# Query and key pieces batch by batch, last expert rows as high and low products, ten idle products at the gate

## The chip, the cores and the metric

One Trainium2 chip, one core. The metric is device time of one execution in microseconds. The engines run side by side and meet at semaphores: TensorE (PE; PEld is its weight load), VectorE (DVE), ScalarE (ACT), GpSimd (POOL), and SyncE (SP), which only issues DMAs here.

## The reference, cut to what matters

1024 tokens of width 256 (two batches of 512) go through two layers. Layer 0 has attention whose 16 heads use unrotated halves and rotated copies of low-rank queries and keys, then a mixture of 16 gated experts. Layer 1 has a gated delta rule, then this mixture of 12 experts, three per token:

```python
for e in range(E):
    sel = top_idx == e
    mask = sel.any(axis=-1)
    cnt = sel.sum()
    w_e = jnp.sum(jnp.where(sel, ew, 0.0)) / jnp.maximum(cnt, 1).astype(ew.dtype)
    h = jax.nn.relu(jnp.einsum('bsh,hi->bsi', x, w1[e]) + b1[e])
    h = jnp.einsum('bsi,ih->bsh', h, w2[e]) + b2[e]
    out = out + mask[..., None].astype(x.dtype) * (w_e * h)
pooled = out.mean(axis=1)
phi = jax.nn.sigmoid(jax.nn.relu(pooled @ Wp1 + bp1) @ Wp2 + bp2)
phi_mask = (phi > 0.7).astype(out.dtype)[:, :, None]
return out * (1.0 - phi_mask * 0.8)
```

An expert's weight is one number, the mean gate of all its tokens. The pooled mean over a batch decides a factor on all its rows.

## The kernel before, in words

Each engine runs its own list of instructions, in the order in which the program writes them; a wait holds everything behind it on that engine.

**Start.** TensorE computes the latents batch by batch (L1163), then eight up-products (L1168 to L1171) in the order of operands 0, 2, 1, 3: unrotated queries, unrotated keys, and their swapped partners. ScalarE copies operands 0 and 2 out (L830). Score products run in bf16 on three pieces of every fp32 number: ScalarE writes the high piece (L821), VectorE the remainder (L1784), ScalarE the middle piece (L825), VectorE the low one (L1788), each over both batches at once. SyncE writes the six piece arrays to DRAM (L546 to L553), waits for all six, and reads them back in the row order that the heads need; ScalarE issues batch 0's query rows (L837). VectorE makes the swapped operands (L1778) and GpSimd the rotation (L690, L692), whose pieces follow the same way. TensorE computes the value products (L1176) and then, once VectorE has read the swapped operands out of PSUM, the modulation of both layers (L1188), which ScalarE copies (L840) and TensorE turns (L1194). Six idle products (`warm`, bf16, 512 columns each) stand before the first score product (L1211). VectorE reduces each score tile to row maxima (L1819).

**Gate.** Behind layer 1's attention, VectorE computes gate logits, the top three, ranks, and a table of token per slot. TensorE adds the gates of each expert over all tokens (L1623, the gate product), VectorE turns them into expert weights and multiplies these into the one-hot table of experts per token (L2414), TensorE transposes that table (L1626), two idle products, and the expert loop begins. The loop has 35 tiles of 128 slots: GpSimd gathers the tokens' rows (L775), TensorE transposes them (L1634), multiplies up (L1645) and down (L1655) in fp32, VectorE adds the bias and clips (L2450) and scales by the expert weight (L2425), GpSimd scatters the rows to DRAM (L781). Down-product r waits for the scaled rows of r - 1, and VectorE's list has the scaling of r - 1 ahead of the activations of r.

**Tail.** The last two tiles aren't scattered. TensorE adds them, and the bias b2 by the transposed table, into PSUM by fp32 products with one-hot matrices (L1660, L1687). SyncE loads the three z rows of every token back (L667) once all scatters have landed, and VectorE adds PSUM and the three rows per pair of token tiles (L2463, L2465, L2466). TensorE pools (L1695), and the small head (L1700, L1703) and the last scaling follow.

F32R is an fp32 number rounded for TensorE; a product in it takes one instruction where fp32 takes two. Layer 0's mixture already uses it with a high and a low part (L1332).

Of the kernel before, what the change touches and what calls it, by code (L numbers as in the profile page):

```python
# [60 lines left out]
NLAST = 2  # L61
# [73 lines left out]
def program(nc, a, out):  # L135
    with ExitStack() as ctx:
# [12 lines left out]
        x_tok = sb("x_tok", [P, NT, D])  # L149
        hT = sb("hT", [P, KD, TOK])  # L150
# [276 lines left out]
        wmT = carve(TOK)  # L427
# [4 lines left out]
        last_hot = arena[:, at[0] - NP1 * P // 2 - NP1 * NT1:][:, 0:NLAST * TOK].rearrange("p (n t k) -> p n t k", n=NLAST, t=NT)  # L432
        assert NLAST * TOK <= NP1 * P // 2 + NP1 * NT1
# [22 lines left out]
        assert at[0] <= ARENA  # L456
# [70 lines left out]
        def _(sp):  # L527
# [35 lines left out]
            parts_out(1)  # L563
# [112 lines left out]
        def _(pool):  # L676
# [11 lines left out]
            for n in range(2):  # L688
                for b in range(B):
# [3 lines left out]
                                       ALU.add).then_inc(s["rotated"], 1)  # L693
            for n in range(2):
                pool.wait_ge(s["part1"], n + 3)
                pool.tensor_tensor(rest[2 * n + 1], X[:, 2 * n + 1, :], pieces[:, 2 * n + 1, 0, :],
                                   ALU.subtract).then_inc(s["rest1"], 1)
            for n in range(2):
                pool.wait_ge(s["part2"], n + 3)
                pool.tensor_tensor(pieces[:, 2 * n + 1, 2, :], rest[2 * n + 1], pieces[:, 2 * n + 1, 1, :],  # L700
                                   ALU.subtract).then_inc(s["part3"], 1)
            pool.wait_ge(s["parts_out0"], 16 * 6)
# [90 lines left out]

        @block.scalar
        def _(act):
# [24 lines left out]
            def first_piece(t):  # L820
                act.activation(pieces[:, t, 0, :], X[:, t, :], ACT.Copy).then_inc(s["part1"], 1)  # L821

            def second_piece(t, count):
                act.wait_ge(s["rest1"], count)
                act.activation(pieces[:, t, 1, :], rest[t], ACT.Copy).then_inc(s["part2"], 1)  # L825

            for n in range(2):
                for b in range(B):
                    act.wait_ge(s["up"], 2 * n + b + 1)
# [4 lines left out]
            for n in range(2):  # L834
# [9 lines left out]
            for n in range(2):  # L844
                second_piece(2 * n + 1, n + 3)
# [1760 lines left out]
```

## Time and profile before

| | us |
|---|---|
| timed runs | 832.76, 833.20, 840.58 |
| their median | 833.2 |
| the profiled execution | 831.77 |
| its span, first to last instruction | 829.9 |

What lies around the span is 1.87. Rows of a timeline give the start and the duration in us, engine, line, operation, output and inputs with shapes, how many were merged (x), and in brackets the idle time before and what ended it.

### The profile page before, as it was taken

Reading aid. Unit: us, or ns where it says so; the run is one execution under the profiler, and the core shown is the slowest. Engines: PE = TensorE matmul, PEld = TensorE weight load, DVE = VectorE, ACT = ScalarE, POOL = GpSimd, SP = SyncE. Lnnn points to the kernel's source line nnn. Section 1 sums busy time; section 2 is a strip of 40 time slices with the busy share of each in tenths; the row PEclk is TensorE's granted clock in tenths of the full one; section 3 lists DMA queues with packets and bytes.
Section 4 is the critical chain, followed back from the end, with each engine's and each line's share of the span. In section 5 each row is a group of like instructions: output and inputs, shape, how many; then the busy total and the mean of one; then the engine's idle time right before and its main releaser. Section 6 shows DMA issues by size and latency. Waiting matters only on the chain. (4 is left out here: it accounts for less than half of the span.)

```text
span 829.9 us, 11442 instructions
## 1 busy us (share of the span) xinstructions
PE 762.5 (92%) x3982; PEld 560.9 (68%) x3982; DVE 538.8 (65%) x1312; ACT 265.2 (32%) x414; POOL 215.6 (26%) x187
## 2 busy tenths in 40 slices
PE   5899999989999999999999498998957999999995
PEld 4422333477788888887456387777734999999985
DVE  4599996458555544455799999998666443434336
ACT  2455778343334434343571111121231000000000
POOL 4470000032223222231030000976002344444410
PEclk9989999979999999999999799999976999999997
DMA  8695000110111111140022405200015899999953
GB/s 293 154 210 96 2 2 3 39 39 20 58 38 57 38 57 38 57 153 1 25 90 77 190 1 171 59 1 1 1 51 189 310 351 344 335 347 346 337 191 109
DMA packets 38516, 101.17 MB, mean 122 GB/s; under 512 B 5294, under 2 KB 18278, under 8 KB 37510
## 3 DMA queue, kind: packets, MB, share of 16 engines
q1 hardware_dynamic: 34470, 91.06, 33.9%
q0 software_dynamic: 3552, 9.11, 2.9%
q10 hardware_dynamic: 448, 0.39, 0.2%
q8 instruction: 27, 0.44, 0.2%
q14 instruction: 19, 0.16, 0.1%
HBM read 84.17 MB, written 16.57 MB: 121 GB/s over the span
## 5 line engine op out<-in xcount | busy, mean ns | idle before, releaser
L1332 PE MATMUL psum<-xr,wr 128*128 128x512 f32 x600 | 145.9, 393 | 1.0 <-DVE arena L1969 1.0
L1332 PEld LDWEIGHTS psum<-xr,wr 128*128 128x128 f32 x600 | 113.9, 190 | 25.4 <-issue 1.7
L720 POOL TENSOR_TENSOR wr<-ring,wr 128x512 fp32r<-128x512 f32 (+1 forms) x50 | 55.0, 1120 | 257.2 <-ACT wr L888 257.2
L1645 PEld LDWEIGHTS psum<-arena 128*128 128x128 f32 x700 | 85.2, 195 | 3.4 <-issue 1.7
L1819 DVE TENSOR_REDUCE small<-psum 128x1 f32<-128x512 f32 x128 | 80.9, 685 | 9.3 <-PE psum L1211 8.4
L1645 PE MATMUL psum<-arena 128*128 128x128 f32 x700 | 85.6, 278 | 1.1 <-issue 0.6
L1655 PE MATMUL psum<-arena 128*128 128x256 f32 x350 | 81.4, 380 | 0.2 <-issue 0.2
L2425 DVE TENSOR_SCALAR arena<-psum,arena 128x256 f32<-128x256 f32 x35 | 16.9, 484 | 98.3 <-PE psum L1655 98.3
L1343 PE MATMUL psum<-hr,wr 128*128 128x512 f32 x300 | 76.6, 391 | 0.9 <-DVE hr L1906 0.9
L1932 DVE TENSOR_TENSOR hid<-hid,psum 128x512 f32<-128x512 f32 x50 | 34.4, 688 | 59.9 <-ACT hid L894 59.7
L867 ACT ACTIVATE arena<-psum 128x1024 f32<-128x1024 f32 x64 | 63.0, 1024 | 27.2 <-PE psum L1221 26.4
L1655 PEld LDWEIGHTS psum<-arena 128*128 128x128 f32 x350 | 63.8, 190 | 7.8 <-issue 0.6
L1343 PEld LDWEIGHTS psum<-hr,wr 128*128 128x128 f32 x300 | 56.2, 188 | 13.0 <-issue 1.3
L1095 ACT ACTIVATE arena<-psum 128x256 f32<-128x256 f32 x35 | 13.5, 385 | 154.5 <-PE psum L1645 79.9
L1906 DVE TENSOR_TENSOR hr<-hid,hr 128x512 fp32r<-128x512 f32 x50 | 35.0, 701 | 34.1 <-ACT hr L901 33.9
L901 ACT ACTIVATE hr<-hid 128x512 fp32r<-128x512 f32 x50 | 31.7, 634 | 78.5 <-DVE hid L1955 68.4
L781 POOL DMA_INDIRECT z_scratch<-arena x33 | 32.7, 990 | 86.8 <-DVE arena L2425 86.8
L775 POOL DMA_INDIRECT arena<-h_scratch,arena x35 | 35.5, 1015 | 69.8 <-DVE arena L2402 59.4
L2450 DVE TENSOR_SCALAR arena<-psum,arena 128x128 f32<-128x128 f32 x175 | 48.3, 343 | 5.3 <-PE psum L1645 5.3
L1211 PE MATMUL psum<-arena 96*128 96x512 bf16 x128 | 46.1, 402 | 1.5 <-DVE small L1819 0.8
L894 ACT ACTIVATE hid<-psum 128x512 f32<-128x512 f32 x50 | 30.0, 600 | 46.1 <-PE psum L1332 45.9
L1211 PEld LDWEIGHTS psum<-arena 96*128 96x128 bf16 x128 | 12.3, 99 | 43.7 <-DVE small L1819 30.2
(379 smaller groups left out, 1213.3 us busy)
## 6 DMA issues: line engine op xcount, KB each, us to landing
arena<-in_w1u SPq DMA_DIRECT2D x35, 642.5 KB
arena<-in_w1d SPq DMA_DIRECT2D x35, 640.0 KB
ring<-in_w SPq DMA_DIRECT2D x25, 384.0 KB, 3.0
part_scratch<-arena SPq DMA_DIRECT2D x12, 256.0 KB, 4.3
z_scratch<-w_a SPq DMA_DIRECT2D x4, 768.0 KB, 7.2
arena<-z_scratch SPq DMA_DIRECT2D x8, 384.0 KB, 6.5
arena<-part_scratch SPq DMA_DIRECT2D x9, 256.0 KB, 7.7
qkv_scratch<-arena SPq DMA_DIRECT2D x4, 512.0 KB, 2.7
```

The lines of the kernel that those rows point to most:

```text
L720: pool.tensor_tensor(wr0[:, k, LO, part], ring0[:, k, part], wr0[:, k, HI, part], ALU.subtract).then_inc(s["w0_lo"], 1)
L775: pool.indirect_dma_start(xg[:, r % NXG, :], None, h_dram, bass.IndirectOffsetOnAxis(ap=tok_i[:, r:r + 1], axis=0))\
L867: act.activation(pexp[:, lo:lo + 2, :], psum[:, 2 + p % 2 * 2:4 + p % 2 * 2, :], ACT.Exp, scale=HD ** -0.5).then_inc(s["exp"], 1)
L1211: pe.matmul(to, Qt[t][0:KR, j, b * S + qt * P:b * S + (qt + 1) * P], Kt[t][0:KR, j, half(b)], start=True, stop=True).then_inc(s["bank_full ...
L1332: ins = pe.matmul(bank[2 * b + m][:, :], wr0[:, k, w, lo:lo + P], xr[:, x, f, half(b)], start=(f == 0 and (w, x) == PARTS[0]), stop=(f == ...
L1343: ins = pe.matmul(bank[4 + 2 * m + b][:, :], wr0[:, k, w, lo:lo + P], hr[:, b, x, :], start=(first and (w, x) == PARTS[0]), stop=(last and ...
L1645: ins = pe.matmul(bank[2 + r % 2 * 3 + k // 2][:, tile(k % 2)], wup1[:, r % NW, lo:lo + P], xgT[:, r % 2, f, :], start=(f == 0), stop=(f = ...
L1655: ins = pe.matmul(bank[1][:, 0:D], hact[:, r % 2, tile(k)], wdn1[:, r % NW, k * D:(k + 1) * D], start=(k == 0), stop=(k == NC1 - 1))
L1819: dve.tensor_reduce(nm[:, g % 2, at16:at16 + 1], full("scores", n), AX, ALU.max, negate=True).then_inc(s["bank_free"], 1)
L1906: dve.tensor_tensor(hr[:, b, LO, :], hid[:, 2 + b, :], hr[:, b, HI, :], ALU.subtract).then_inc(s[f"{name}_lo"], 1)
L1932: return dve.tensor_tensor(hid[:, 2 + b, :], hid[:, b, :], bank[2 * b + 1][:, :], ALU.mult)
L2450: ins = dve.tensor_scalar(hact[:, r % 2, tile(k)], bank[2 + r % 2 * 3 + k // 2][:, tile(k % 2)], bias, 0.0, ALU.add, ALU.max)
```

## The change

Start: everything on unrotated queries and keys is done per batch, batch 0 first (copies, pieces, writes); TensorE's up-products are ordered by unrotated or swapped, then by batch, and wait for one batch's latents each; the modulation products stand ahead of the value products and wait for two swapped operands. Gate: five idle products ahead of the gate product, one behind it, four instead of two behind the transposes; the table of experts per token gets three blocks (high, low, high), and b2 three matching blocks. Tail: the last three tiles stay on the chip instead of two; their rows and the bias are multiplied as F32R, the rows in a high part (ScalarE) and a low part (VectorE); bias and the first of these tiles stand ahead of down-product 34, the others behind it; GpSimd adds two of the three z rows, VectorE the third, and PSUM comes last. Buffers and PSUM banks move accordingly, and the pieces of b2 are prepared by VectorE ahead of the logits.

```diff
-NLAST = 2
+NLAST = 3
+LAST_BANKS = (5, 6, 7, 0)
...
-            def parts_out(pair):
+            def parts_out(pair, before, own):
                 for part in range(3):
                     for n in range(2):
-                        sp.wait_ge(s[f"part{part + 1}"], 2 * pair + n + 1)
-                        load(f"parts_out{pair}", part_dram[n, pair, part], pieces[:, 2 * n + pair, part, :])
-            parts_out(0)
+                        sp.wait_ge(s[f"part{part + 1}"], before + n + 1)
+                        load(f"parts_out{pair}", part_dram[n, pair, part][:, own], pieces[:, 2 * n + pair, part, own])
+            parts_out(0, 0, half(0))
             sp.wait_ge(s["parts_out0"], 16 * 6)
-            for b in range(B):
-                k_rows(sp, 0, half(b), rows_in(0, b))
+            k_rows(sp, 0, half(0), rows_in(0, 0))
+            parts_out(0, 2, half(1))
+            sp.wait_ge(s["parts_out0"], 16 * 6 * B)
+            k_rows(sp, 0, half(1), rows_in(0, 1))
             q_rows(sp, 0, half(1), rows_in(0, 1))
             def all_rows(t):
                 k_rows(sp, t, slice(0, TOK), rows_in(t, 0))
                 q_rows(sp, t, slice(0, TOK), rows_in(t, 0))
             all_rows(1)
-            parts_out(1)
+            parts_out(1, 2 * B, slice(0, TOK))
+            sp.wait_ge(s["v_mm"], NT // 2)
             sp.wait_ge(s["parts_out1"], 16 * 6)
             all_rows(2)
...
+            for i in range(0, NT, 2):
+                pool.wait_ge(s[Z_IN[i // 2][0]], Z_IN[i // 2][1] + 16 * 2)
+                pool.tensor_tensor(acc1[:, i:i + 2, :], zt[:, i:i + 2, 0, :], zt[:, i:i + 2, 1, :], ALU.add)\
+                    .then_inc(s["z_pair"], 1)
...
+                for n in range(2):
+                    act.wait_ge(s["up"], 2 * b + n + 1)
                     act.activation(X[:, 2 * n, half(b)], bank[4 * b + 2 * n][:, :], ACT.Identity,
                                    bias=cols[:, BUP + 2 * n:BUP + 2 * n + 1]).then_inc(s["up_copy"], 1)
-                act.wait_ge(s["up_copy"], 2 * n + 2)
-                first_piece(2 * n)
-            for n in range(2):
-                second_piece(2 * n, n + 1)
+                for n in range(2):
+                    act.wait_ge(s["up_copy"], 2 * b + n + 1)
+                    first_piece(2 * n, half(b))
+                for n in range(2):
+                    second_piece(2 * n, 2 * b + n + 1, half(b))
             act.wait_ge(s["parts_out0"], 16 * 6)
             q_rows(act, 0, half(0), rows_in(0, 0))
+            act.wait_ge(s["part3"], 3)
             act.wait_ge(s["mod_mm"], 2)
             for x in range(2):
                 act.activation(mod_rows[:, x, :], bank[1 + 2 * x][:, :], ACT.Copy).then_inc(s["mod_rows"], 1)
...
+            for n in range(NLAST):
+                r = NT1 - NLAST + n
+                act.wait_ge(s["y1"], r + 1)
+                act.activation(last_y[:, n, HI, :], yb[:, r % 3, :], ACT.Copy).then_inc(s["xgT"], 1)
...
-            pe.wait_ge(s["lat_in"], 2)
-            for t in (0, 2, 1, 3):
+            for pair in range(2):
                 for b in range(B):
-                    pe.matmul(bank[4 * b + t][:, :], wup[:, t, :], lat[:, half(b)],
-                              start=True, stop=True).then_inc(s["up"], 1)
+                    pe.wait_ge(s["lat_in"], b + 1)
+                    for t in (pair, 2 + pair):
+                        pe.matmul(bank[4 * b + t][:, :], wup[:, t, :], lat[:, half(b)],
+                                  start=True, stop=True).then_inc(s["up"], 1)
+            pe.wait_ge(s["ones"], 2)
+            pe.wait_ge(s["swapped"], 2)
+            pe.wait_ge(s["ld_mod1"], 32)
+            for n in range(MODC):
+                layer, lo = (0, 2 * D + 512 * n) if n < 2 else (1, 512 * (n - 2))
+                for k in range(KD):
+                    ins = pe.matmul(bank[1 + n // 4 * 2][n % 4 * Q:n % 4 * Q + B, :], ccol[:, layer * KD + k, :],
+                                    wmod[layer][:, k, lo:lo + 512], start=(k == 0), stop=(k == KD - 1))
+            ins.then_inc(s["mod_mm"], 1)
...
+            warm(5, 7)
             pe.wait_ge(s["routed"], 8)
             pe.matmul(bank[5][:, 0:E1], ones, sums, start=True, stop=True).then_inc(s["routing_pe"], 1)
+            warm(1, 7)
             pe.wait_ge(s["routed"], 9)
...
-            warm(2, 1)
+            def sums_of(i):
+                return bank[LAST_BANKS[i // 2]][:, i % 2 * D:(i % 2 + 1) * D]
+            def bias_rows():
+                for i in range(NT):
+                    pe.matmul(sums_of(i), bias_w[:, tile(i)], b2r[:, :],
+                              start=(i % 2 == 0), stop=False, skip_group_check=True)
+            def last_rows(n):
+                pe.wait_ge(s["routed"], 10 + NLAST + n + 1)
+                for i in range(NT):
+                    for x in (HI, LO):
+                        ins = pe.matmul(sums_of(i), last_hot[:, n, i, :], last_y[:, n, x, :], start=False,
+                                        stop=(n == NLAST - 1 and x == LO), skip_group_check=True)
+                    if n == NLAST - 1 and i % 2:
+                        ins.then_inc(s["routing_pe"], 1)
+            warm(4, 1)
...
                 if r == NT1 - 1:
                     pe.wait_ge(s["wmT"], B)
-                    pe.wait_ge(s["ld_wp"], 16 * LD_WP)
-                    for i in range(NT // 2, NT):
-                        bias_rows(i)
+                    pe.wait_ge(s["act1"], NT1 - 1)
+                    pe.wait_ge(s["xgT"], NT1)
+                    bias_rows()
+                    pe.wait_ge(s["routed"], 10 + NLAST)
+                    last_rows(0)
                 down1(r)
...
+            for n in range(1, NLAST):
+                last_rows(n)
...
             dve.wait_ge(s["ld_cs"], 16)
+            first_rest(0, 0)
+            first_rest(2, 0)
+            third_piece(0, 0)
+            third_piece(2, 0)
+            swapped(0, 0)
+            swapped(0, 1)
             first_rest(0, 1)
-            swapped(0, 0)
-            first_rest(2, 2)
+            first_rest(2, 1)
+            swapped(1, 0)
             third_piece(0, 1)
-            third_piece(2, 2)
-            swapped(1, 0)
-            for b in range(B):
-                swapped(b, 1)
+            swapped(1, 1)
+            third_piece(2, 1)
...
+            dve.memset(wmp, 0.0)
             dve.wait_ge(s["ld_wp"], 16 * LD_WP)
+            ch.link(dve.tensor_copy(b2h[:, :], b2))
+            ch.link(dve.tensor_copy(b2r[:, :], b2))
+            ch.link(dve.tensor_tensor(b2r[64:96, :], b2[64:96, :], b2h[64:96, :], ALU.subtract))
...
-            dve.tensor_tensor(wmp[:, :, 0:E1], hot, we.unsqueeze(1).broadcast_to((P, NT, E1)),
-                              ALU.mult).then_inc(s["routed"], 1)
+            by_w = we.unsqueeze(1).broadcast_to((P, NT, E1))
+            dve.tensor_tensor(wm, hot, by_w, ALU.mult)
+            ch.link(dve.tensor_tensor(wm_hi[:, :, :], hot, by_w, ALU.mult))
+            for n in (0, 64):
+                dve.tensor_copy(wmp[:, :, n:n + E1], wm_hi[:, :, :])
+            dve.tensor_tensor(wmp[:, :, 32:32 + E1], wm, wm_hi[:, :, :], ALU.subtract).then_inc(s["routed"], 1)
...
+            def last_low(n):
+                r = NT1 - NLAST + n
+                dve.wait_ge(s["y1"], r + 1)
+                dve.wait_ge(s["xgT"], NT1 + n + 1)
+                dve.tensor_tensor(last_y[:, n, LO, :], yb[:, r % 3, :], last_y[:, n, HI, :],
+                                  ALU.subtract).then_inc(s["routed"], 1)
...
-                if r:
+                if 0 < r < NT1 - 1:
                     rows_out(r - 1)
...
+                if r == NT1 - 2:
+                    last_low(0)
+            rows_out(NT1 - 2)
+            last_low(1)
+            def z_third(i):
+                dve.wait_ge(s["z_pair"], i // 2 + 1)
+                dve.wait_ge(s[Z_IN[i // 2][0]], Z_IN[i // 2][1] + 16 * 2)
+                summed.append(ch.mark(dve.tensor_tensor(acc1[:, i:i + 2, :], acc1[:, i:i + 2, :], zt[:, i:i + 2, 2, :],
+                                                        ALU.add)))
+            summed = []
+            for i in range(0, NT // 2, 2):
+                z_third(i)
             rows_out(NT1 - 1)
+            last_low(2)
+            for i in range(NT // 2, NT, 2):
+                z_third(i)
             for i in range(0, NT, 2):
-                both = acc1[:, i:i + 2, :]
                 dve.wait_ge(s["routing_pe"], i // 2 + 5)
-                dve.wait_ge(s[Z_IN[i // 2][0]], Z_IN[i // 2][1] + 16 * 2)
-                ch.link(dve.tensor_tensor(both, zt[:, i:i + 2, 0, :], bank[4 + i // 2].rearrange("p (t n) -> p t n", t=2),
-                                          ALU.add))
-                ch.link(dve.tensor_tensor(both, both, zt[:, i:i + 2, 1, :], ALU.add))
-                dve.tensor_tensor(both, both, zt[:, i:i + 2, 2, :], ALU.add).then_inc(s["mixed"], 1)
+                ch.need(summed[i // 2])
+                dve.tensor_tensor(acc1[:, i:i + 2, :], acc1[:, i:i + 2, :],
+                                  bank[LAST_BANKS[i // 2]].rearrange("p (t n) -> p t n", t=2), ALU.add)\
+                   .then_inc(s["mixed"], 1)
```

## Rows read from the trace of the kernel before

**Rows 1.** The page: busy time of each engine over the span.

```profile
PE 762.5 (92%) x3982; PEld 560.9 (68%) x3982; DVE 538.8 (65%) x1312; ACT 265.2 (32%) x414; POOL 215.6 (26%) x187
```

**Rows 2.** Timeline of the start, 20 to 41 us.

```profile
20.45 7.13 PE L1170 MATMUL psum<-arena,w_a 128*128 128x512 f32 x16 [0.84 <-DVE arena L1774]
...
23.19 1.06 ACT L821 ACTIVATE arena<-arena 128x1024 bf16<-128x1024 f32 x1
...
27.42 3.62 PE L1176 MATMUL psum<-w_a,arena 128*128 128x256 f32 x16
...
27.67 2.44 DVE L1788 TENSOR_TENSOR arena<-arena 128x1024 bf16<-128x1024 f32 x2
...
32.34 3.59 PE L1188 MATMUL psum<-arena,ccol 128*2 128x512 f32 x20 [1.31 <-DVE hT L1778]
...
33.15 1.80 ACTq L523 DMA_DIRECT2D arena<-part_scratch  x4
...
38.04 1.46 PE L1139 MATMUL psum<-sel,identb 128*128 128x512 bf16 x6
...
40.17 0.38 PE L1211 MATMUL psum<-arena 96*128 96x512 bf16 x1 [0.67 <-DMA arena<-part_scratch]
```

**Rows 3.** Timeline of the gate, 615 to 649 us.

```profile
615.76 0.26 DVE L2339 TENSOR_TENSOR rt<-psum,rows 128x96 f32<-128x96 f32 x1 [0.85 <-PE psum L1591]
...
635.83 0.60 PE L1623 MATMUL psum<-arena 128*128 128x12 f32 x2 [2.65 <-DVE arena L2409]
...
637.06 1.97 PE L1626 MATMUL psum<-ident,arena 128*128 128x128 f32 x8 [0.63 <-DVE arena L2414]
...
639.72 0.29 PEld L1634 LDWEIGHTS psum<-ident,arena 128*128 128x128 f32 x2 [0.74 <-DMA arena<-h_scratch,arena]
...
640.98 4.16 PE L1645 MATMUL psum<-arena 128*128 128x128 f32 x20 [0.57 <-issue]
...
645.92 2.47 PE L1645 MATMUL psum<-arena 128*128 128x128 f32 x20 [0.57 <-ACT arena L1095]
```

**Rows 4.** Windows; the last three columns are granted clock, DMA share, GB/s.

```profile
630.00:632.00 2.00, 1.70 (x19) 0.92 (x16) 2.00 (x2) 0.00 (x0) 0.00 (x0) 1.00 0.36 90
634.00:636.00 2.00, 0.17 (x1) 0.17 (x2) 1.76 (x10) 0.00 (x0) 1.05 (x1) 0.57 1.02 392
812.00:814.00 2.00, 2.00 (x11) 1.75 (x10) 1.72 (x3) 0.00 (x0) 0.00 (x0) 1.00 0.32 96
```

**Rows 5.** Timeline of the tail, 801 to 821 us.

```profile
801.57 5.38 SPq L529 DMA_DIRECT2D arena<-z_scratch  x8
...
802.52 1.89 PE L1660 MATMUL psum<-ring,arena 128*128 128x256 f32 x8
...
804.60 2.40 PE L1655 MATMUL psum<-arena 128*128 128x256 f32 x10 [0.19 <-issue]
...
811.15 4.48 PE L1687 MATMUL psum<-arena 128*128 128x256 f32 x20
812.21 0.69 DVE L2463 TENSOR_TENSOR arena<-arena,psum 128x512 f32<-128x512 f32 x1 [0.45 <-PE psum L1687]
...
815.47 2.73 PE L1695 MATMUL psum<-arena 128*128 128x1 f32 x24
...
820.35 0.16 DVE L2468 TENSOR_SCALAR arena<-psum 128x4 f32<-128x4 f32 x1 [1.90 <-PE psum L1695]
```

**Rows 6.** Timeline of layer 0, where VectorE meets GpSimd and where not.

```profile
166.13 1.39 DVE L1732 TENSOR_SCALAR xn<-x_tok,mv,rstd 128x256 f32<-128x256 f32 x4
...
170.06 2.74 DVE L1732 TENSOR_SCALAR xn<-x_tok,mv,rstd 128x256 f32<-128x256 f32 x4
170.17 2.16 POOL L720 TENSOR_TENSOR wr<-ring,wr 128x512 fp32r<-128x512 f32 x2 [107.94 <-ACT wr L888]
```

**Rows 7.** The page: groups of instructions, the F32R products.

```profile
L1332 PE MATMUL psum<-xr,wr 128*128 128x512 f32 x600 | 145.9, 393 | 1.0 <-DVE arena L1969 1.0
L1332 PEld LDWEIGHTS psum<-xr,wr 128*128 128x128 f32 x600 | 113.9, 190 | 25.4 <-issue 1.7
```

More of the change, by code:

```diff
@@ L149, in program @@
         x_tok = sb("x_tok", [P, NT, D])
+        hT_at = nc.sbuf_base
         hT = sb("hT", [P, KD, TOK])
@@ L842, in _ @@
                 act.wait_ge(s["rotated"], 2 * n + 2)
-                first_piece(2 * n + 1)
+                first_piece(2 * n + 1, slice(0, TOK))
             for n in range(2):
-                second_piece(2 * n + 1, n + 3)
+                second_piece(2 * n + 1, 2 * B + n + 1, slice(0, TOK))
             def max_in(j):
@@ L1165, in _ @@
                 ins.then_inc(s["lat"], 1)
-            pe.wait_ge(s["lat_in"], 2)
-            for t in (0, 2, 1, 3):
+            for pair in range(2):
                 for b in range(B):
-                    pe.matmul(bank[4 * b + t][:, :], wup[:, t, :], lat[:, half(b)],
-                              start=True, stop=True).then_inc(s["up"], 1)
-            pe.wait_ge(s["up_copy"], 4)
-            for m in range(NT // 2):
-                for x in range(2):
-                    ins = pe.matmul(bank[2 * m][:, x * D:(x + 1) * D], lat[:, tile(2 * m + x)], wv,
-                                    start=True, stop=True)
-                ins.then_inc(s["v_mm"], 1)
-            pe.wait_ge(s["identb"], 1)
+                    pe.wait_ge(s["lat_in"], b + 1)
+                    for t in (pair, 2 + pair):
+                        pe.matmul(bank[4 * b + t][:, :], wup[:, t, :], lat[:, half(b)],
+                                  start=True, stop=True).then_inc(s["up"], 1)
             pe.wait_ge(s["ones"], 2)
-            pe.wait_ge(s["swapped"], 4)
+            pe.wait_ge(s["swapped"], 2)
             pe.wait_ge(s["ld_mod1"], 32)
@@ L1190, in _ @@
             ins.then_inc(s["mod_mm"], 1)
+            pe.wait_ge(s["up_copy"], 4)
+            for m in range(NT // 2):
+                for x in range(2):
+                    ins = pe.matmul(bank[2 * m][:, x * D:(x + 1) * D], lat[:, tile(2 * m + x)], wv,
+                                    start=True, stop=True)
+                ins.then_inc(s["v_mm"], 1)
+            pe.wait_ge(s["swapped"], 4)
             pe.wait_ge(s["mod_rows"], 2)
@@ L1657, in down1 @@
                 ins.then_inc(s["down1"], 1)
-            def bias_rows(i):
-                pe.matmul(bank[4 + i // 2][:, i % 2 * D:(i % 2 + 1) * D], wmT[:, tile(i)], b2,
-                          start=(i % 2 == 0), stop=False, skip_group_check=True)
-            warm(2, 1)
+            def sums_of(i):
[13 more added lines that the diff above has]
+            warm(4, 1)
             gathered(0)
@@ L1694, in _ @@
                 for f in range(KD):
-                    ins = pe.matmul(bank[2 * b + f][:, 0:1], acc1[:, i, tile(f)], ones[:, 0:1],
+                    ins = pe.matmul(bank[1 + 2 * b + f][:, 0:1], acc1[:, i, tile(f)], ones[:, 0:1],
                                     start=(i % TB == 0), stop=(i % TB == TB - 1))
@@ L1699, in _ @@
             for k in range(KD):
-                ins = pe.matmul(bank[4][:, 0:B], wp[:, tile(k)], pooled[:, k, :], start=(k == 0), stop=(k == KD - 1))
+                ins = pe.matmul(bank[5][:, 0:B], wp[:, tile(k)], pooled[:, k, :], start=(k == 0), stop=(k == KD - 1))
             ins.then_inc(s["phi_mm"], 1)
             pe.wait_ge(s["phi_act"], 1)
-            pe.matmul(bank[5][:, 0:B], wp2b, phi[:, 0, :], start=True, stop=True).then_inc(s["phi_mm"], 1)
+            pe.matmul(bank[6][:, 0:B], wp2b, phi[:, 0, :], start=True, stop=True).then_inc(s["phi_mm"], 1)
         @block.vector
@@ L2566, in lay_out @@
     r["b2"] = np.zeros((P, D), f)
-    r["b2"][:E1] = i["L1_ffn_b2"]
+    for n in (0, 32, 64):
+        r["b2"][n:n + E1] = i["L1_ffn_b2"]
     up = i["L1_ffn_w1"].reshape(E1, KD, P, I1).transpose(0, 2, 1, 3).reshape(E1, P, KD * I1)
```

70 lines of the change are left out of this document (31 added, 39 removed).

## The prediction

> **What bounds the kernel now.** I read the page first: TensorE is busy 92% of the span [rows 1], so only a place where TensorE waits, runs at half clock, or does work that could be cheaper is worth anything. The reader sees three such places in the timelines, and the change touches these three.
>
> At the start, attention's first score product begins at 40.17, released by the DMA that brings query and key rows back [rows 2]. Two chains end there within 0.7 us. One is data: the last piece is written at 27.67 + 2.44 = 30.11, the six writes to DRAM have landed at 33.15 when ScalarE issues its reads, and the reads land 7.0 later. The other is TensorE's own: it waits 1.31 for VectorE, computes the modulation products from 32.34 to 35.93, and its transposes and fillers end at 38.04 + 1.46 = 39.50.
>
> At the gate, TensorE has been idle for 2.65 when the gate product comes at 635.83 [rows 3], and the granted clock falls from 1.00 in 630 to 632 to 0.57 in 634 to 636 [rows 4]; 0.50 is the 1.2 GHz level. The eight transposes then take 1.97, and the first tile's twenty up-products 4.16 where the next tile's twenty take 2.47 [rows 3].
>
> In between, the expert loop is pure TensorE. At the end TensorE still runs fp32 bias and one-hot products to 811.15 + 4.48 = 815.63, VectorE makes three additions of 0.69 per pair of token tiles, and the pooled means leave TensorE at 820.35 [rows 5]. All behind 820.35 (9.55 to the end of the span) is untouched.
>
> **Start.** Each whole-width piece operation becomes two halves, batch 0 first. A half costs VectorE 0.69 (the 512-wide addition, [rows 5]) and ScalarE about 0.6, estimated from 1.06 for the whole [rows 2]. The up-products run 0.86 apart per product (eight in 7.13, with their tail) and wait for batch 0's latents alone, so the 0.84 of waiting before 20.45 goes: they start near 19.4. Batch 0's two unrotated products come out at about 20.6 and 21.4. ScalarE's two copies and two high pieces end at 23.4, VectorE's two remainders at 24.3, the middle pieces at 24.9, the low pieces at 25.7: 4.4 earlier than 30.11. ScalarE's reads stand behind its batch-1 pieces in its queue, so they go out near 29.1 instead of 33.15, and batch 0's rows land near 36.1 if they take 7.0 as before. They now compete with the writes of batch 1 instead of the reads of batch 1.
> TensorE's chain: the modulation products are moved ahead of the value products and wait for two swapped operands, which VectorE has at 25.7 + 2 x 0.75 = 27.2 (0.75 estimated from the same 0.69). 3.59 of modulation [rows 2], 3.62 of value products behind them, then the transposes (1.1, an estimate from the eight at the gate) and the six fillers (1.4) end at 36.9. VectorE's value additions end at 35.2 and hold nothing. So the start is 36.9 instead of 40.17: **-3.2**, and what is late next is TensorE's own order. Bounds: -4.1 (the rows set it) and -1.0 (the reads take 2.2 longer in the new mix of transfers). Batch 1's rows leave SyncE only after its own writes have landed, near 35, and are wanted when VectorE has reduced batch 0's sixteen score tiles: hidden. GpSimd's rotation still waits for all four swapped halves, and its rows are wanted four groups later.
>
> **Gate.** Ahead of the logits VectorE gets three linked operations on 256 columns, 0.35 each (four in 1.39, [rows 6]); it idles 0.85 there [rows 3]: +0.2, bounds 0 and +0.6. One 96-wide product becomes five operations of 0.26 or less (a 96-wide one, [rows 3]), partly overlapped: +0.8 on the way to the transposes, which start at 637.9. Of the ten fillers the first five (1.1 at full clock) run from 633.2 to 634.3 and the sixth behind the gate product, both in idle time. If the clock stays up, the transposes take about 1.0, four fillers 0.86 and the gathered rows, whose DMA lands at 639.72 [rows 3], set the next step; the up-products then take 2.47 for 4.16. That ends 2.3 before the present 645.14. If the level falls anyway, the transposes and four slow fillers (1.7 instead of 0.85) are 1.7 late, less what an earlier rise gives back. Between -2.3 and +1.7 I take **-1.0** with the 0.8 inside, since the fillers fill less than half of the idle time.
> The Trainium skill, TensorE: Matmul & The Clock Gate, section Part 1 (The HAM clock gate), says that the count of slow products differs from run to run of one kernel. By that this term is a draw between its two ends rather than a fixed number; by the rows of this one execution alone it would be nearer to the gain.
>
> **Tail.** A high/low product has no width of 256 in the trace. The 600 F32R products of 512 columns occupy 145.9, 0.24 each [rows 7]; half of that is 0.12, an fp32 product of 256 columns (two instructions of ten in 2.40) is 0.48 at most [rows 5]. I take 0.12, as the 512-wide ones cost by column; bounds 0.12 and 0.48.
> VectorE no longer puts the rows of tile 33 ahead of tile 34's activations, so down-product 34 isn't held to 804.60 by them; but 8 bias and 16 last-row products (2.9) now stand ahead of it from 802.52: it starts at 805.4, +0.8, and ends at 807.9. Tile 33's 16 products follow (1.9, to 809.7). Tile 34's rows need 0.5 for the scaling and about 0.4 each for the high copy on ScalarE and the low part on VectorE (estimated from 1.06 for 1024 and 0.69 for 512 columns): 809.3, so TensorE hardly waits; its last 16 end near 811.5 instead of 815.63.
> The z loads start behind scatter 31 instead of 32, one tile earlier than 801.57 [rows 5], 4.6 by the twenty up-products (2.47, [rows 3]) and ten down-products (2.40) less their overlap; the data now end in 812 to 814 [rows 4], so they will end near 808.6. GpSimd adds the first two of each pair, 1.1 each (two in 2.16, [rows 6]); the last is ready at 809.7.
> Four z additions leave the end of the chain; four remain at 0.69 each. One collision is counted: where four VectorE operations on SBUF met GpSimd's, they took 2.74 instead of 1.39 [rows 6]. Here the low part of tile 34 meets the last GpSimd addition: +0.9. So VectorE's last four run from 811.7 to 814.5, and the pooling products, 0.91 a pair (24 in 2.73, [rows 5]), end at 816.1 instead of 820.35: **-4.2**; -5.0 without the collision.
> The Trainium skill, GPSIMD Engine Reference, section 1, says that GpSimd shares its SBUF interfaces with VectorE and contends with its operations of two SBUF inputs or in a two-port mode. The trace agrees as far as it goes (2.74 for 1.39).
>
> The sum is -3.2 + 0.2 - 1.0 - 4.2 = -8.2, made against the profiled execution's own 831.77: 823.6. The median of the runs shown is 833.2, 1.4 higher; I put the forecast between 823.6 and 825.0, at 824.3.
>
> **Rivals.** (a) The start gives 1.0 because the reads take 2.2 longer in the new mix, and the F32R weight loads don't hide behind 256 columns (0.19 each, [rows 7], instead of 0.12): +2.2 and +1.4, about 828. For it: the weight loads' own mean is above 0.12, and the reads already took 7.0. Against it: at 29 fewer transfers are in flight than at 33, and fp32 weight loads followed each other faster than their mean (twenty products in 2.47, [rows 3]).
> (b) The clock stays up through the gate and GpSimd's last addition misses the low part: -1.3 and -0.8, about 822.
> (c) The other side: F32R products of 256 columns go as slowly as fp32 ones. There are 56 of them in the tail, one behind the other, and the pooled means leave at 806.7 + 56p. With p = 0.48 that is 833.6, 13.2 later than now, and the total is 831.77 - 4.0 + 13.2 = 841. It decides from p = 0.31 on, where the total equals today's. For it: no product of that kind and width is in the trace; against: the wide ones go by column at a quarter of the fp32 price.
> (d) The z additions hold the last rows: tile 34's scaling stands behind two z additions on VectorE. By the sum they are done near 806, two before the scaling is due; from there each us that the second pair lands later costs one. With loads that end as late as today, near 813 [rows 4], the last z addition and all behind it come 3 later: 827.
> That the split pieces or the fillers do nothing is within (a) and the gate's bounds.
>
> **Numbers.** Forecast 0.60, (a) 0.17, (b) 0.11, (c) 0.05, (d) 0.07. A difference under 1% (8.3) is what a measurement of this kernel can't tell from none. The forecast's -8.9 to -8.2 lies on that line: by half of it and all of (b) the change is faster by more, by the other half, (a) and (d) it is within, and (c) with a disturbed measurement (0.02) is slower. Faster 0.50, same 0.43, slower 0.07. The range 820 to 831 takes in (a), (b) and (d) with the uncertainty of the gate, and leaves out (c).
>
> **What would show it.** First score product near 36.9 and released by TensorE's own order, not by the DMA; last unrotated piece of batch 0 near 25.7; transposes at the gate near 1.0 with a granted clock of 1.00 in the first up-products (or 0.50, which is the bad draw); 16 last-row products in about 1.9; pooled means some 8.2 earlier. Wrong would be: a first score still behind its reads, F32R products over 0.2 each, or VectorE's last four additions behind a DMA.

## The result, and the profile after

The changed kernel took 829.82 us (median of 12 executions, 828.66 to 831.75), the kernel before 835.91 beside it (12 executions, 830.28 to 840.58): a ratio of 0.994 [0.9917, 0.9963], some 5 us less. The forecast was 824.3: a sum of 8.2 less than the execution its rows come from, lifted by 0.7. The time fell inside the range, but a third of the gain is missing, and the time is 5.5 above the forecast.

The profiled execution took 828.66, with a span of 826.5 (829.9 before). First, in the timeline of the start, the rows that answer to [rows 2]:

```profile
20.14 7.03 PE L1194 MATMUL psum<-arena,w_a 128*128 128x512 f32 x16
...
24.75 1.29 DVE L1821 TENSOR_TENSOR arena<-arena 128x512 bf16<-128x512 f32 x2
...
27.47 3.59 PE L1204 MATMUL psum<-arena,ccol 128*2 128x512 f32 x20 [0.30 <-issue]
...
29.08 1.86 ACTq L530 DMA_DIRECT2D arena<-part_scratch  x4
...
30.99 3.72 PE L1211 MATMUL psum<-w_a,arena 128*128 128x256 f32 x16
...
34.55 1.04 PE L1219 MATMUL psum<-ident,arena 128*128 128x128 f32 x8
...
36.87 0.38 PE L1236 MATMUL psum<-arena 96*128 96x512 bf16 x1
```

Batch 0's low pieces end at 24.75 + 1.29 = 26.04 (25.7 by the working), ScalarE's reads go out at 29.08 (29.1), and the first score stands at 36.87 (36.9) with no DMA behind it: 3.3 earlier than 40.17. This part came as worked out. Then, 10 us further on in the same view, where nothing was priced:

```profile
44.54 4.20 POOL L711 TENSOR_TENSOR arena<-arena 128x1024 bf16<-128x1024 f32 x2
45.67 1.28 DVE L1856 TENSOR_REDUCE small<-psum 128x1 f32<-128x512 f32 x2
...
46.98 1.80 DVE L1862 CAST mpart<-small 128x16 bf16<-128x16 f32 x1
...
48.81 0.18 DVE L1863 TENSOR_TENSOR mpart<-small,mpart 128x16 bf16<-128x16 f32 x1
...
49.04 0.63 PE L1273 MATMUL psum<-identb,mpart 128*2 128x128 bf16 x16 [3.22 <-DVE mpart L1863]
...
65.63 0.30 SPq L536 DMA_DIRECT2D max_scratch<-max_sb  x1
...
68.95 0.79 SPq L536 DMA_DIRECT2D arena<-max_scratch  x1
...
71.19 0.60 PE L1246 MATMUL psum<-arena 98*128 98x512 bf16 x2 [2.87 <-DMA arena<-max_scratch]
```

Once batch 0's sixteen score tiles are reduced, VectorE casts sixteen columns of row maxima; the cast ends only when GpSimd's second piece subtraction does (44.54 + 4.20 = 48.74). In the kernel before the same two instructions took 0.17 each, since the maxima came after GpSimd was done (45.36 + 4.20 = 49.56):

```profile
45.36 4.20 POOL L700 TENSOR_TENSOR arena<-arena 128x1024 bf16<-128x1024 f32 x2
...
50.27 0.17 DVE L1825 CAST mpart<-small 128x16 bf16<-128x16 f32 x1
50.48 0.17 DVE L1826 TENSOR_TENSOR mpart<-small,mpart 128x16 bf16<-128x16 f32 x1
50.71 0.63 PE L1248 MATMUL psum<-identb,mpart 128*2 128x128 bf16 x16 [1.60 <-DVE mpart L1826]
```

Being 3.3 early has moved them under it, for GpSimd's subtractions came only 0.8 earlier. TensorE waits 3.22 for the maxima's transposes, and of 3.3 only 50.71 - 49.04 = 1.7 is left. The lower rows of the changed kernel are a second stall, treated below.

At the gate (timeline, [rows 3]):

```profile
634.42 1.24 PE L1162 MATMUL psum<-sel,identb 128*128 128x512 bf16 x5
...
637.23 0.39 PE L1649 MATMUL psum<-arena 128*128 128x12 f32 x2 [1.58 <-DVE arena L2449]
...
638.95 1.97 PE L1653 MATMUL psum<-ident,arena 128*128 128x128 f32 x8 [1.10 <-DVE arena L2459]
...
640.71 1.71 PE L1162 MATMUL psum<-sel,identb 128*128 128x512 bf16 x4
...
643.21 2.47 PE L1672 MATMUL psum<-arena 128*128 128x128 f32 x20 [0.57 <-issue]
...
646.46 2.47 PE L1672 MATMUL psum<-arena 128*128 128x128 f32 x20 [0.56 <-ACT arena L1113]
```

Its windows there, with the columns of [rows 4]:

```profile
636.00:638.00 2.00, 0.62 (x3) 0.32 (x3) 1.58 (x9) 0.00 (x0) 1.56 (x2) 1.00 1.00 403
...
640.00:642.00 2.00, 2.00 (x9) 1.09 (x8) 0.63 (x2) 0.00 (x0) 1.68 (x2) 0.50 0.68 177
```

With the five fillers (the idle products) the granted clock is 1.00 up to 638 (0.57 before in 634 to 636, [rows 4]); it is 0.50 in 640 to 642, so transposes and four fillers are slow, and back when the first tile's up-products come: 2.47 for 4.16. The way from the gate product to the transposes grew from 1.23 to 1.72: five operations for one.

At the end (timeline, [rows 5]):

```profile
802.87 1.30 PE L1691 MATMUL psum<-b2r,bias_w 128*128 128x256 f32 x8
...
807.61 1.28 POOL L807 TENSOR_TENSOR arena<-arena 128x512 f32<-128x512 f32 x1 [0.97 <-DMA arena<-z_scratch]
807.90 4.17 PE L1698 MATMUL psum<-last_y,last_hot 128*128 128x256 f32 x32
...
809.80 1.70 POOL L807 TENSOR_TENSOR arena<-arena 128x512 f32<-128x512 f32 x1 [0.91 <-DMA arena<-z_scratch]
811.54 0.69 DVE L2516 TENSOR_TENSOR arena<-arena 128x512 f32<-128x512 f32 x1 [1.18 <-POOL arena L807]
812.15 2.47 DVE L2529 TENSOR_TENSOR arena<-arena,psum 128x512 f32<-128x512 f32 x4
...
812.88 4.03 PE L1727 MATMUL psum<-arena 128*128 128x1 f32 x32 [0.81 <-DVE arena L2529]
816.95 0.16 DVE L2533 TENSOR_SCALAR arena<-psum 128x4 f32<-128x4 f32 x1 [2.33 <-PE psum L1727]
```

An F32R product of 256 columns takes 4.17/32 = 0.13. The last addition on GpSimd first waits 0.91 for its z rows to land, then takes 1.70 where its fellows took about 1.27, and VectorE waits 1.18 for it before its last four additions. From the second tile's up-products to the pooled means it is now 816.95 - 646.46 = 170.5, where it was 820.35 - 645.92 = 174.4: 3.9 less.

### The profile page after: what moved, and what is told of

It reads as the page before. It is cut to its first block and busy times, and to the rows that moved or that the text cites. A ratio compares the mean times of both kernels' runs of the same rounds, so it can differ in the third digit from the quotient of the medians.

```text
span 826.5 us, 11512 instructions
## 1 busy us (share of the span) xinstructions
PE 758.8 (92%) x3998; PEld 556.6 (67%) x3998; DVE 543.9 (66%) x1323; ACT 266.6 (32%) x421; POOL 221.0 (27%) x190
## 5 line engine op out<-in xcount | busy, mean ns | idle before, releaser
L1672 PEld LDWEIGHTS psum<-arena 128*128 128x128 f32 x700 | 83.5, 192 | 3.3 <-issue 1.5
L1672 PE MATMUL psum<-arena 128*128 128x128 f32 x700 | 83.9, 275 | 1.1 <-issue 0.6
L1682 PEld LDWEIGHTS psum<-arena 128*128 128x128 f32 x350 | 63.8, 190 | 7.2
```

The lines of the kernel that those rows point to most:

```text
L1672: ins = pe.matmul(bank[2 + r % 2 * 3 + k // 2][:, tile(k % 2)], wup1[:, r % NW, lo:lo + P], xgT[:, r % 2, f, :], start=(f == 0), stop=(f = ...
L1682: ins = pe.matmul(bank[1][:, 0:D], hact[:, r % 2, tile(k)], wdn1[:, r % NW, k * D:(k + 1) * D], start=(k == 0), stop=(k == NC1 - 1))
```

## The experiments

Two theories stood after this. A: the start's gain is given back in attention. B: one profile against one profile misleads. To hold them apart I timed the parts alone and together and took a profile of each. Two tables first; the text under each experiment refers to them. The "fillers" are the added idle products. Times are means over all executions of a kernel, with the standard error of the mean:

```
kernel                                 executions  mean us
before                                     99      834.8 +- 0.25
start alone                                12      831.3 +- 0.6
tail alone (two timings)                   24      833.1 +- 0.6
tail and fillers                           12      832.7 +- 0.6
start and tail                              7      828.8 +- 0.7
all: the changed kernel (two timings)      18      829.4 +- 0.4
changed, maxima reduced instead of cast     6      828.5 +- 0.6
changed, GpSimd kept apart (two timings)   12      826.4 +- 0.6
changed, apart, bias operations moved       7      828.2 +- 0.8
```

From each profile's timeline: when the first score starts (a); from it to the maxima's transposes (b); from them to layer 0's router, the gate product of its mixture (c); from layer 1's first logits to the second tile's up-products (d); from these to the end of the span (e); and, as a part of c, from the issue of the second group's write of row maxima to DRAM to that of their reading behind it (w). The stretch between c and d, which the change doesn't touch, is left out; it takes 433.7 to 437.0, and 433.7 in the changed kernel's first profile where the rows' own execution has 435.7:

```
profile                   a      b      c       d      e      w
before (the rows used)   40.17  10.54  122.42  37.08  183.99  1.3
before, again            40.78  10.55  127.14  38.44  183.96  3.1
before, third            40.63  10.55  129.25  33.99  183.23  3.5
tail alone               41.35  10.55  123.69  37.44  179.57  1.3
tail alone, again        40.37  10.54  127.03  36.23  180.36  3.0
tail and fillers         40.09  10.54  126.82  34.12  180.25  3.1
start alone              36.37  12.18  126.85  36.84  183.27  3.1
start and tail           36.09  12.18  127.14  36.85  180.05  3.3
changed                  36.87  12.17  127.06  36.67  180.05  3.3
changed, again           36.67  12.17  126.25  40.20  180.20  3.2
changed, maxima reduced  35.94  11.97  126.61  34.84  180.54  3.1
apart                    36.37  10.55  122.51  37.23  179.84  1.9
apart, again             35.91  10.55  126.68  37.25  180.07  3.1
apart, bias moved        36.48  10.55  122.25  37.25  179.95  1.4
```

**Start alone.** The kernel before with the start's parts of the diff and nothing else:

```diff
-            parts_out(0)
+            parts_out(0, 0, half(0))
...
-            for t in (0, 2, 1, 3):
+            for pair in range(2):
...
```

> The kernel before with the start's change alone. Theory A (given back in attention): the time of the kernel before, its median of 835.9 within 1.0, with a first score near 37 and a cast of the first row maxima above 1 us in the profile. Theory B (the gain carries through): 3.3 less, 832.6.

Median 830.96, ratio 0.9963 [0.9942, 0.9983]. The time speaks for B, the profile for A: the cast took 1.80 at 46.48. The collision is there and yet the time falls by 3.6 +- 0.7 in the mean; the later profiles of the kernel before show how both can be.

**Changed, without the fillers.**

```diff
-            warm(5, 7)
...
-            warm(1, 7)
...
-            warm(4, 1)
+            warm(2, 1)
```

> The changed kernel without the eight added filler products at the gate product and the transposes (five, one and two; the two old ones stay). If the fillers bring what the profile shows (first tile's up-products 2.47 instead of 4.16, less about 0.9 for two more fillers), 0.5 to 1.7 more than the changed kernel: 830.3 to 831.5, with twenty up-products of about 4.2 at a granted clock of 0.50. If the level at that place is a draw in both, the same time within 0.5.

Median 829.13, ratio 0.9936 [0.991, 0.9962]: no slower than with them. Its first tile's up-products took 2.47 too, with no filler near the gate product. Over all profiles, they took 2.47 in four of seven without fillers and 4.16 to 4.61 in three; with fillers 2.47 in six of seven, and 4.61 in the changed kernel's second profile. So the level there differs from one execution to the next; that the fillers better its odds is possible, but no time shows it (d).

**Changed, GpSimd kept apart.** The last piece subtraction waits for the first maxima, the memsets for the second:

```diff
             for n in range(2):
+                if n:
+                    pool.wait_ge(s["mpart"], 1)
                 pool.wait_ge(s["part2"], 2 * B + n + 1)
...
             pool.wait_ge(s["parts_out1"], 16 * 6)
+            pool.wait_ge(s["mpart"], 2)
```

> The changed kernel with GpSimd kept out of VectorE's way: its last piece subtraction waits until the first row maxima are written, and its two memsets until the second are. Theory A (collision): the cast of the maxima takes 0.2 instead of 1.80 and the second 0.2 instead of 0.89, the maxima's transposes come 1.6 earlier, and the time falls by 1.5 to 2.5, to 827.3 to 828.3. Theory B (the collisions are absorbed later, by the reading of the row maxima): no difference from the changed kernel, 829.8 within 0.5. The pieces leave about 1 us later; if their rows are then late for the third group of scores, the time rises.

Median 827.05, ratio 0.992 [0.9893, 0.9947]. In its timeline GpSimd's second subtraction stands behind the maxima, and the cast is short:

```profile
44.05 2.13 POOL L713 TENSOR_TENSOR arena<-arena 128x1024 bf16<-128x1024 f32 x1
...
46.49 0.17 DVE L1865 CAST mpart<-small 128x16 bf16<-128x16 f32 x1
46.69 0.17 DVE L1866 TENSOR_TENSOR mpart<-small,mpart 128x16 bf16<-128x16 f32 x1
...
46.92 0.43 PE L1276 MATMUL psum<-identb,mpart 128*2 128x128 bf16 x16 [1.60 <-DVE mpart L1866]
46.95 2.12 POOL L713 TENSOR_TENSOR arena<-arena 128x1024 bf16<-128x1024 f32 x1 [0.77 <-DVE mpart L1866]
```

Column b is 10.55 in all nine profiles without the collision and 11.97 to 12.18 in all five with it: about 1.6, and no draw.

**The changed kernel again**, unaltered, beside the next three.

> The changed kernel once more, unaltered, beside the next three and the kernel before on one chip: 829.8 within 1.0. Its profile shows how far one execution's picture holds: a cast of the first row maxima of 1.8 (by the collision, in every execution), and the write of the next row maxima with a 16 KB code block ahead of its last packets (a stall of TensorE of about 2.9 where the kernel before has 1.0) if that too comes with the collision; about 1.0 if it was a chance of the one execution.

Median 827.47, ratio 0.991 [0.9879, 0.994], cast and write as in the first profile. By its mean over both timings the change is worth 834.8 - 829.4 = 5.4.

**Changed, with the old start.** The start's hunks taken back (as in the first experiment, the other way round).

> The changed kernel with the start as it was before (whole-width pieces, modulation behind the values; one semaphore on the bfloat16 identity is left out, its wait is covered by a later one); gate and tail stay changed. Theory A (the start's 3.3 is lost again in attention): the time of the changed kernel, 829.8 within 1.0. Theory B (most of it is kept in the mean over executions, as the start's change alone showed with a ratio of 0.9963): 2 to 3.5 more, 831.8 to 833.3.

Median 832.57, ratio 0.9984 [0.9961, 1.0006]. Against the changed kernel's 829.4 the start is worth 3.3 in the mean; theory A in its plain form falls. But its attention took longer than that of the kernel before, from whose code it doesn't differ there: c is 126.82 instead of 122.42.

**Tail alone.** That kernel without the fillers.

> The kernel before with the tail's change alone (high and low parts, three last tiles, additions on GpSimd; with the three operations on the biases and the five at the gate that belong to it, without the fillers and without the start). By the profiles the tail gains 3.95 and the operations at the gate cost 0.45 and 0.5: theory A, 3.0 less than the kernel before, some 831; theory B (the half level of the clock takes part of it back): 1 to 2 less, 832.5 to 833.5.

Median 834.48, ratio 0.9996 [0.9974, 1.0019]: no gain shown by its time, where column e is 4.4 less than in the rows' own execution.

**Apart, bias operations moved.** As the kernel kept apart, and

```diff
-            ch.link(dve.tensor_copy(b2h[:, :], b2))
-            ch.link(dve.tensor_copy(b2r[:, :], b2))
-            ch.link(dve.tensor_tensor(b2r[64:96, :], b2[64:96, :], b2h[64:96, :], ALU.subtract))
...
             ch.link(dve.tensor_reduce(tile_w, past, AX, ALU.add))
+            ch.link(dve.tensor_copy(b2h[:, :], b2))
+            ch.link(dve.tensor_copy(b2r[:, :], b2))
+            ch.link(dve.tensor_tensor(b2r[64:96, :], b2[64:96, :], b2h[64:96, :], ALU.subtract))
```

> The changed kernel with GpSimd kept out of VectorE's way as in the run that did that alone, and the three operations on the biases moved from ahead of the logits to behind the gate chain, where VectorE waits for the first up-products. Theory A: 0.45 less than that run (827.05), 826.6, and the logits' first operation starts as TensorE ends them. Theory B (the gate's chain is absorbed by the fillers and the clock): the same as that run within 0.3.

Median 828.97, ratio 0.9928 [0.99, 0.9955], a mean of 828.2 where 826.6 was looked for; d is 37.25 as in the kernel kept apart. So moving the operations gains nothing: theory B. But GpSimd is kept apart here as well, and beside it the changed kernel took no longer (828.0 +- 0.9).

**The kernel before, twice more.** Unaltered, against itself.

> The kernel before against itself, for a second profile of it. From its first score to layer 0's router, attention took 132.96 in the profile that the prediction used, but 134.24 and 137.36 in the two runs that have the same start (tail alone, no start). Theory A (the 132.96 is what this start gives, and the changed start's 138.4 to 139.3 is a loss of its own): 133 to 134 again. Theory B (the profile used was a lucky draw, and the old start usually loses as much): 136 to 139, and a ratio of 1.000 within 0.003.

> The kernel before once more, one look, for a third profile: theory A 133 to 134 from the first score to the router, theory B 136 to 139.

835.21 and 836.46, a ratio of 0.9993 [0.9965, 1.0021] for the first. Theory B: from the first score to the router 137.7 and 139.8 instead of 132.96, and spans of 837.6 and 834.6 instead of 829.9. The rows that the prediction used are those of a lucky execution, 831.77 where the mean is 834.8. What differs stands in the timelines, first of the rows' own execution, then of the first of the two:

```profile
66.59 0.30 SPq L529 DMA_DIRECT2D max_scratch<-max_sb  x1
...
67.93 0.79 SPq L529 DMA_DIRECT2D arena<-max_scratch  x1
...
70.29 0.60 PE L1221 MATMUL psum<-arena 98*128 98x512 bf16 x2 [1.01 <-DMA arena<-max_scratch]
```

```profile
67.26 0.30 SPq L529 DMA_DIRECT2D max_scratch<-max_sb  x1
...
70.37 0.79 SPq L529 DMA_DIRECT2D arena<-max_scratch  x1
...
72.57 1.03 PE L1221 MATMUL psum<-arena 98*128 98x512 bf16 x2 [2.62 <-DMA arena<-max_scratch]
```

and in the DMA view, first of the changed kernel, 64 to 70 us (a queue's line: packets, MB, share; an issue's line: times issued, KB, us from issue to landing):

```profile
q8 instruction: 1, 0.02, 1.3%
...
max_scratch<-max_sb SPq DMA_DIRECT2D x1, 8.0 KB, 3.3
```

then of the rows' own execution, the same stretch:

```profile
q8 instruction: 1, 0.02, 1.0%
...
max_scratch<-max_sb SPq DMA_DIRECT2D x1, 8.0 KB, 1.3
```

In both a block of 16 KB on the queue of instructions, that is of code, comes just then as a single packet. In the rows' execution it starts at 67.67, after the write's last packet (67.55). In the changed kernel's it starts at 66.51, among the write's 32 packets, takes 1.25, and the last two of them go only at 67.74 and 67.77. The column w divides all fourteen profiles: 1.3 to 1.9 in four, where the block started after the write's last packet; 3.0 to 3.5 in ten, where it started before. With the short write c is 122.7 in the mean, with the long one 127.1; the ten have a stretch of TensorE at half clock between 66 and 82, in or right after its wait for the maxima, and the four have none behind theirs. So 4.4 us of c go with a difference of a few tenths in when the block starts. It fell badly in four of six profiles with the old start, in five of five with the collision, in one of three kept apart; whether the collision makes it likelier can't be told from so few.

**Tail alone, again.**

> The tail's change alone once more, with new timings and a second profile. Its first timing gave a ratio of 0.9996, while its profile shows the stretch from the first tile's second half to the end shorter by 4.4. Theory A (the tail's gain is real in each execution, and a draw of the clock elsewhere hid it): a ratio of 0.995 to 0.997 and again 4 less in that stretch. Theory B (the operations that the tail's change adds at the gate, about 0.95 by the profile, let TensorE idle longer and cost a stretch at half clock more, which takes the gain back): a ratio of 0.998 to 1.000, with 38 or more from the logits to the second tile's up-products where the kernel before has 37.1.

Median 831.03, ratio 0.9977 [0.9949, 1.0004], and e is again 3.6 less than in the rows' execution. d is 36.23, so the extra operations brought no longer way at the gate here. Nearer to A, with a smaller gain.

**Apart, again.**

> The changed kernel with GpSimd kept out of VectorE's way, once more. In its first profile attention from the first score to the router took 133.1 where the changed kernel takes 138.4 to 139.3. Theory A (the collision costs 5 to 6 there in each execution): 133 again, and 826 or less. Theory B (half of it is a draw): 133 to 137 and 827 to 829.

Median 825.11, ratio 0.9905 [0.987, 0.994]. From the first score to the router it took 137.2, with b at 10.55 and w at 3.1: by that stretch theory B, half is a draw, though the time is as low as theory A had it. Over both timings this kernel is 829.4 - 826.4 = 3.0 +- 0.7 faster than the changed one and 8.4 +- 0.6 faster than the one before. Against the changed kernel the size is less sure: the two weren't timed beside each other, and with the seven executions that also have the bias operations moved, the mean of the kernels kept apart is 827.1, 2.3 +- 0.6 faster.

**The cast as a reduction.** One instruction in another form, the same values:

```diff
-                    ch.link(dve.tensor_copy(mpart[:, g % 2, 0, :], nm[:, g % 2, :]))
+                    ch.link(dve.tensor_reduce(mpart[:, g % 2, 0, :], nm[:, g % 2, :].unsqueeze(2), AX, ALU.max))
```

> The changed kernel with one instruction in another form: VectorE's cast of sixteen maxima to bfloat16 is written as a reduction over a one-long axis (the same values); GpSimd's subtractions stay where they are. Theory A (VectorE waits because of the form of its operation: the sixteen reductions from PSUM ahead of it run beside the same GpSimd subtraction undisturbed): the reduction takes 0.2 at about 46.9, and either the subtraction behind it takes the wait of 1.6 instead (it reads two operands from SBUF) and nothing is gained, 829.4 within 1; or that too passes, the transposes come 1.6 earlier and the time is 826 to 828. Theory B (any VectorE operation on SBUF waits there): the reduction itself takes 1.8, and the time is that of the changed kernel.

Median 827.98, ratio 0.992 [0.9892, 0.9948]. Its timeline, GpSimd's row first:

```profile
43.62 4.20 POOL L711 TENSOR_TENSOR arena<-arena 128x1024 bf16<-128x1024 f32 x2
...
46.05 0.17 DVE L1862 TENSOR_REDUCE mpart<-small 128x16 bf16<-128x16 f32 x1
46.25 1.60 DVE L1863 TENSOR_TENSOR mpart<-small,mpart 128x16 bf16<-128x16 f32 x1
47.91 0.63 PE L1273 MATMUL psum<-identb,mpart 128*2 128x128 bf16 x16 [3.03 <-DVE mpart L1863]
```

The reduction passes beside GpSimd's subtraction in 0.17, and the subtraction behind it takes the wait. So the form of VectorE's operation decides (theory A, in its first branch: hardly anything is gained at the transposes, b is 11.97). The Trainium skill, SBUF — State Buffer, section Who interferes with whom, says just this: casts and copies can meet GpSimd on the shared ports, an operation with two SBUF inputs meets GpSimd's reads, and a reduction never does. These rows agree (1.80, 1.60 and 0.17).

## Why the prediction was right and wrong

**Start.** Right up to the first score: 36.87 for 36.9, in the order worked out. The times on the way were near it: the up-products began at 20.14 for 19.4, the low pieces ended 0.3 late, and the reads that were to land at 36.1 had landed by 34.1, so TensorE's own order decided, as said. What failed is the step that carried -3.2 undiminished to the end. Behind 37 us it asked for batch 1's rows and for the rotated rows, not for the maxima on VectorE: these came 3.3 earlier and met GpSimd's piece subtractions, which had moved by 0.8. That returned 1.6 in every profile that had both, and keeping GpSimd apart took it away in all three. The collision was priced where the change adds GpSimd operations (the tail), not where it moves VectorE under old ones. Rival (a) had the start at 1.0, by slower reads; those didn't come. That the first score moved by just 3.3 was luck of the base: over the profiles it comes at 40.6 in the six with the old start and at 36.3 in the eight with the new, 4.2 earlier.

**Gate.** The -1.0 + 0.2 was taken between -2.3 and +1.7 from one execution; over the profiles d has a mean of 36.6 in the four without tail and fillers, 36.8 in the three with the tail alone and 36.8 in the seven with both. Single profiles lie between 34.0 and 40.2, so a gain of 0.8 isn't excluded, but none is shown, nor by the times (829.4 with the fillers, 828.8 +- 0.7 without). The rows showed 4.16 for 2.47 as if it were the rule; in seven profiles without fillers over 4 came three times.

**Tail.** 3.9 by the profile against 4.2. The products went as named: 0.13 for an F32R product (0.12 taken; rival (c) began at 0.31 and fell). The path at the very end was another. The z rows of the last pair landed just before 809.80 where near 808.6 was worked out (0.5 of it because the second tile's up-products came 0.5 later), and a GpSimd addition takes 1.27 where 1.1 was taken; so VectorE's last four additions stood behind a DMA and a GpSimd addition, which the prediction had named as a sign of being wrong. It is rival (d) in a milder form: tile 34's scaling wasn't held. The collision that was counted there doesn't decide: GpSimd's last addition took 1.5 to 1.75 in four of the ten profiles with the tail and 1.28 to 1.37 in six, and in the changed kernel's second profile, where it took 1.30, e is 180.20 instead of 180.05. That the tail's 4.2 came out near, by another path, is luck in this part. Over all profiles e goes from 183.6 to 180.1, 3.5 less. By time the tail alone gains 1.7 +- 0.6, and 2.5 +- 1.0 on top of the start. What takes the rest in time isn't shown: the operations added at the gate (0.45 ahead of the logits, 0.5 behind the gate product) lengthen the profile used, but d doesn't show them in the mean. This stays open.

**Base.** The sum was made against 831.77 and lifted by 0.7 toward a median of three; the mean of 99 is 834.8. So 8.2 less would have been 826.6, and 2.3 of the 5.5 by which the time was missed are the base alone. Another 2.8 is the difference between 8.2 and the 5.4 that the change brings. By the profiles, 1.6 of it are the collision and 0.8 the gate, with 0.4 within the error of the mean. By the times of the parts the split is another: the start brings 3.6 +- 0.7 alone and 3.3 +- 0.7 with the rest, no less than its 3.2, the fillers nothing, and the tail 1.7 to 2.5 where 4.2 was forecast. The collision is shown and so are its 1.6, but that it is what the total lacks isn't: draws elsewhere are as large, and how the 2.8 divide stays open. The last 0.4 lies between the first timing's median and the mean over both. With the collision taken out the gain is 8.4 +- 0.6, the sum that was forecast; that is luck, since the gate's part is missing from it, part of it is the better draw of the maxima's write, and with the bias operations moved it was 6.7 +- 0.8.

## What to carry to other kernels

When a stage is brought forward, walk on past its end and ask which engine pairs now overlap that didn't: here the collision came 10 us behind the first score product, up to which the start was worked out. A late GpSimd operation that nobody waits for soon can be held back by one wait, and that was worth some 2 to 3 us, about what the change's gate and tail gave together (2.1 +- 0.6 with the old start). And take the base of a sum, and any term that rests on a clock level, from several profiles of the kernel before: two more would have shown that its attention takes 133 or 138 to 140.

## What the runs showed of the hardware that was not expected

A VectorE cast of 128x16 waited 1.6 behind a GpSimd operation that had begun before it; a memset on GpSimd does it as well: the second cast took 1.45 at 61.80 in the third profile of the kernel before, under memsets from 56.27 to 63.23.

A fetch of 16 KB of code can hold up the kernel's own small writes. The 8 KB write takes 1.3 to 1.9 to its next step when all its packets go ahead of the block and 3.0 to 3.5 when the block starts before the last of them. In nine of these ten profiles two packets are held for 0.85 to 1.3, until the block ends; that they share one of the 16 DMA engines with it is inferred from this. In the tenth (kept apart, again) no packet is held like that, and the last goes 0.3 after the block's start. So the hold explains a part; why SyncE went on only 1.1 to 1.2 after the last packet in all ten (0.3 to 0.9 in the other four) is not explained. That the rest of the 4.4 is the stretch at half clock is read from where it stands, not tried.
